# Set-up of a gated expert layer: matrix products moved from VectorE to GpSimd, TensorE and ScalarE

## The reference, cut to what matters

```
x = x + ga * attn(layernorm(x) * (1 + ca) + sa)        # 8 batches of 1024 tokens, width 128, 8 heads
h = layernorm(x) * (1 + cb) + sb
x = x + gb * ffn(h)

def ffn(h):
    gates = softmax over the 2 best of 8 experts of h[:, 0, :] @ Wr.T     # one row of gates per batch
    mid = einsum('blh,erh->belr', h, A)
    expert_out = einsum('belr,ehr->belh', mid, Bw)
    return h + einsum('be,belh->blh', gates, expert_out)
```

## Time and profile before

| | us |
|---|---|
| median of 3 runs | 816.1 (813.3 to 819.37) |
| the profiled execution, its own time | 814.3 |
| its span | 812.5 |
| mean granted TensorE clock in it | 0.958 of full speed |

### The profile page before, as it was taken

The page is one execution under the profiler, slowest core; times in us unless marked ns, Lnnn a source line. Parts: engine busy times, 40 slices in busy tenths (PEclk is TensorE's granted clock), DMA queues, the critical chain, the costliest instruction groups (busy, mean ns, idle before and its releaser), DMA issues.

```text
span 812.5 us, 21167 instructions
## 1 busy us (share of the span) xinstructions
PE 705.3 (87%) x4437; PEld 577.8 (71%) x4437; DVE 759.0 (93%) x6490; ACT 678.9 (84%) x2182; POOL 465.8 (57%) x871
## 2 busy tenths in 40 slices
PE   5987989999898889988988899889888998898844
PEld 3445667777777777777777777777777777777743
DVE  5956899999999999999999999999999999999980
ACT  3981359988888998898989988898999888988964
POOL 2112456666666666666666666666666666666541
PEclk9995989999999999999999999999999999999955
DMA  5310000111111001111110011111100111111000
GB/s 171 107 31 10 25 17 27 32 32 32 33 31 31 27 26 32 32 32 32 31 31 27 26 32 33 33 31 31 31 25 29 32 31 32 32 31 31 19 4 10
DMA packets 49232, 27.23 MB, mean 34 GB/s; under 512 B 5513, under 2 KB 48593, under 8 KB 49105
## 3 DMA queue, kind: packets, MB, share of 16 engines
q1 hardware_dynamic: 49104, 25.90, 10.9%
HBM read 10.28 MB, written 4.19 MB: 18 GB/s over the span
## 4 chain that ended last, share of the span: by engine, by line
DVE 83%; PE 9%; ACT 2%; DMA 2%; issue 1%; POOL 1%; SPq 1%; ACTq 0%; POOLq 0%
DVE work L990 46%; DVE m L979 30%; DVE key L1012 5%; DMA big<-in_x 1%; PE psD L1145 1%; DVE key L801 1%; PE psD L1050 1%; DVE st_p L792 1%; PE psC L1175 1%; PE psC L1078 1%; PE psW L1232 1%; PE psW L1161 1%; DMA wmod_sb<-in_wmod 1%; POOL big L452 1%; PE psX L1133 0%
## 5 line engine op out<-in xcount | busy, mean ns | idle before, releaser
L990 DVE MATCH_REPLACE8 work<-m,work 128x64 f32<-128x64 f32 x1536 | 301.0, 208 | 0.0
L1145 PE MATMUL psD<-sst,tst 128*128 128x224 f32 x1024 | 238.7, 356 | 0.0
L979 DVE MAX8 m<-work 128x8 f32<-128x64 f32 x1536 | 211.5, 210 | 0.0
L1145 PEld LDWEIGHTS psD<-sst,tst 128*128 128x128 f32 x1024 | 196.5, 192 | 3.1 <-issue 0.3
L452 POOL TENSOR_TENSOR big<-work,con 128x512 f32<-128x512 f32 x128 | 162.2, 1290 | 20.5 <-ACT work L635 15.9
L481 POOL TENSOR_TENSOR t<-cst,qh 128x128 f32<-128x128 f32 x64 | 27.7, 433 | 213.2 <-ACT cst L715 213.2
L1175 PE MATMUL psC<-vst,big 128*128 128x34 f32 x1024 | 127.5, 270 | 0.0
L1175 PEld LDWEIGHTS psC<-vst,big 128*128 128x128 f32 x1024 | 126.8, 195 | 0.2
L990 DVE MATCH_VALUE_LOAD work<-m,work 128x8 f32 x1536 | 122.3, 80 | 0.0
L990 DVE MATCH_REPLACE8 work<-m,key 128x64 f32<-128x64 f32 x512 | 100.2, 208 | 0.0
L1142 PE MATMUL psD<-mask_bf,ident_bf 128*128 128x448 bf16 x256 | 91.5, 357 | 1.8 <-DMA tst<-nst 1.8
(11 more groups left out here) (200 smaller groups left out, 1473.6 us busy)
## 6 DMA issues: line engine op xcount, KB each, us to landing
hst<-hT_all SPq DMA_DIRECT2D x64, 96.0 KB
tst<-qT_all SPq DMA_DIRECT2D x256, 17.0 KB
big<-in_x SPq DMA_DIRECT2D x16, 256.0 KB, 2.8
tst<-nst SPq DMA_DIRECT2D x256, 1.0 KB
xs<-in_x SPq DMA_DIRECT2D x64, 64.0 KB, 1.9
out<-yo SPq DMA_DIRECT2D x64, 64.0 KB, 1.7
sst<-nst SPq DMA_DIRECT2D x128, 3.0 KB
con<-in_consts SPq DMA_DIRECT2D x1, 549.5 KB, 6.7
```

Of the source, the lines that this page charges most:

```text
L979: last = v.max(m8[:, h], src[:, h * WIN:(h + 1) * WIN])
L990: last = v.match_replace(work[:, s, cols], m8[:, h], src[:, cols], GONE)
L1145: last = mm(bank_of(r)[:, g, 0:SW], tst[:, s, r, g], sst[:, s, g], start=False, stop=(g == NG - 1), skip_group_check=True)
```

## The change

- DVE: both `bsc` products, and `expert_matrices` with both its calls, are taken out.
- POOL: `routing(0)` makes all four `bsc`. In `step(1)`, after `unfold(1)`, it multiplies the two halves of `g_b` by `mI`, each after the copy on ACT.
- PE: `routing(0)` adds the identity by one more product per bank (identity by identity repeated four times, 128 x 512).
- ACT: `routing(1)` copies the two banks to `mI`, 128 x 512 each, ahead of its `step(1)`.
- `mI` has room for both halves. PE's `contexts(0)` of step 1 waits for the two copies; the wait for `gb_ready` moves to the first use of `g_b`, in step 3.

```
--- before.py
+++ after.py
@@ buffers and semaphores
-        mI = sb("mI", [P, 4, D])
+        mI = sb("mI", [P, 2, 4, D])
+        mI_ready = sem("mI_ready")
@@ POOL, step(i), behind unfold(1)
+                if i == 1:
+                    for half in range(2):
+                        four = slice(4 * half, 4 * half + 4)
+                        pool.wait_ge(mI_ready, half + 1)
+                        nc.gpsimd.tensor_tensor(g_b[:, four], g_b[:, four], mI[:, half], ALU.mult).then_inc(gb_ready, 1)
@@ POOL, routing(0)
-                    for kt in range(2, 4):
+                    for kt in range(4):
                         nc.gpsimd.tensor_tensor(bsc[:, kt], b_sb[:, kt].unsqueeze(1).broadcast_to([P, NB, D]),
@@ ACT, routing(i)
+                if i == 1:
+                    for half, bank in enumerate((psC, psX)):
+                        act.wait_ge(pG_ready, half + 1)
+                        nc.scalar.activation(mI[:, half].rearrange("p b d -> p (b d)"), bank[:], ACT.Copy).then_inc(mI_ready, 1)
@@ DVE, routing(i)
-                if i == 0:
-                    dve.wait_ge(r0_dve, 10)
-
-                    for kt in range(2):
-                        v.tensor_tensor(bsc[:, kt], b_sb[:, kt].unsqueeze(1).broadcast_to([P, NB, D]),
-                                        gate_er[:, kt].unsqueeze(2).broadcast_to([P, NB, D]), ALU.mult).then_inc(bsc_ready, 1)
-                if i == 1:
-                    expert_matrices(0)
-
-            def expert_matrices(half):
-
-                four = slice(4 * half, 4 * half + 4)
-                dve.wait_ge(pG_ready, half + 1)
-                need(dve, gb_ready, half)
-                link(v.tensor_tensor(mI[:], (psC, psX)[half][:].rearrange("p (b d) -> p b d", b=4),
-                                     ident.unsqueeze(1).broadcast_to([P, 4, D]), ALU.add))
-                v.tensor_tensor(g_b[:, four], g_b[:, four], mI[:], ALU.mult).then_inc(gb_ready, 1)
@@ DVE, step(i), behind replaces(i, 0, 1)
-                if i == 1:
-                    expert_matrices(1)
@@ PE, routing(0)
                         for kt in range(4):
-                            last = mm(bank[:], a_sb[:, kt], bsc[:, kt, 4 * half:4 * half + 4].rearrange("p b d -> p (b d)"),
-                                      start=(kt == 0), stop=(kt == 3))
-                        last.then_inc(pG_ready, 1)
+                            mm(bank[:], a_sb[:, kt], bsc[:, kt, 4 * half:4 * half + 4].rearrange("p b d -> p (b d)"),
+                                      start=(kt == 0), stop=False)
+                        mm(bank[:].rearrange("p (b d) -> p b d", b=4), ident, ident.unsqueeze(1).broadcast_to([P, 4, D]),
+                           start=False, stop=True).then_inc(pG_ready, 1)
@@ PE, contexts(0) of step 1
-                                pe.wait_ge(gb_ready, 2)
+                                pe.wait_ge(mI_ready, 2)
@@ PE, step(i), ahead of the product with g_b
+                    if k == 0:
+                        pe.wait_ge(gb_ready, 2)
```

## The result

Over 22 runs each, the changed kernel's median is 816.19 us (814.12 to 820.77) and that of the kernel before 813.67 (811.07 to 819.37). The ratio is 1.0036, with a 95% interval of 1.0018 to 1.0053: 2.9 us slower by this ratio and by the means of the runs, 2.5 us between the two medians, clear of noise, and far from 1%. The forecast was +0.3%.

A forecast was written before the change was run, and what follows sets the result against it. The chain over PE, ACT and POOL, not DVE, bounds the stretch up to chunk 3's L1012. Identity 1.71 + copies 1.10 - unfold 0.44 = 2.37 us; 816.1 + 2.4 = 818.5 us, range 813.0 to 823.0.

The forecast's parts named there:

- DVE has slack, the chain over PE, ACT and POOL bounds the stretch: From 92.33 us to chunk 3's L1012 at 120.84, the 8.3 us taken off DVE all turn into waits.
- The rival of 807.8: DVE is the bound throughout, so its 8.3 us are gained: 816.1 - 8.3 = 807.8 us; chance 0.04.
- bsc on POOL at 1.75 to 1.90 each, free: Four in routing(0) end at 90.6 to 91.2, before PE's first expert product at 92.33; cost 0.
- the -0.44 of the unfold: POOL's first pair of unfolds takes 2.54 for 2.98 us, without DVE's L969 in between.
- estimate of 2.25 us for one bsc: Price on POOL from the skill's 4497 ns for 2048 elements; 0.3 us of wait on PE; not taken.
- Identity 1.71: Two more fp32 products of 0.86 us on PE, before its step 0 on the chain: +1.71 us.
- Copies 1.1: ACT's two bank copies, behind L772 and ahead of L628, go into the chain: 1.0 to 1.2, taken 1.1 us.
- Products with mI covered by POOL's wait: Two behind unfold(1), 2.1 to 3.0 us, covered by POOL's 3.04 us wait for ACT's cst; cost 0.
- The clock as before: PE's fall to 1.2 GHz at 108.65 to 115.40 us stays; up to 2.6 us less or more otherwise.
- DVE's waits 5.0 and 2.5 at chunks 2 and 3: DVE waits 5.0 us for L686 at chunk 2 and 2.5 us at chunk 3's L1012.
- Its signs: Right: DVE busy 8.4 us less, chunk 3's L1012 at 123.2. Wrong: PE's first expert product after 93, among others.

The follow-up runs named there:

- e12: Kernel before with the identity added by PE as in the change and DVE copying the banks where it added; ratio 1.0048 to the kernel before.
- e9: The changed kernel once more, unedited, for a second trace and median; ratio 1.0033 to the kernel before.
- e1: Kernel before with all four bsc products on POOL and none on DVE, nothing else moved; ratio 1.0004 to the kernel before.
- e7: Kernel before with one more 128x512 fp32 product on PE, result unused, in its wait for POOL at the head of step 1; ratio 0.9979.
- e3: Changed kernel with PE's two identity products moved to the end of routing(-1), where PE waits for a DMA; ratio 1.0012 to the kernel before.

## Why the prediction was right

Time, range and direction held: +2.4 us forecast, +2.9 measured, and 816.19 lies in 813 to 823. The forecast of 818.5 stood on a median of 3 runs that was 2.4 above the one of 22; the ratio is what it got right (1.0029 for 1.0036), and the median itself was missed by 2.3. By its steps:

- *DVE has slack, the chain over PE, ACT and POOL bounds the stretch.* Right, and shown from both sides: 5.2 us less DVE work alone change nothing (37.08 for 37.24), 8 us more in the changed kernel change nothing (41.07 for 41.08). The rival of 807.8 is out.
- *bsc on POOL at 1.75 to 1.90 each, free.* Right: each 1.895 or 1.896, 7.46 us for four, 1.2 us ahead of PE. The reading of the durations as turns between DVE and POOL gave the price; their mean of 2.39 would not have. It also bore out the -0.44 of the unfold: 2.52 for 2.98, and 2.50 in e12, where DVE's product with mI ends before the unfold begins. The prediction's estimate of 2.25 us for one bsc was too long: 1.90 is measured. The 4497 ns behind it stand in the Trainium skill, "GPSIMD Engine Reference", in "3.1 Elementwise — side-by-side cycle accounting", and not in the section that the prediction names. The Trainium skill, "SBUF — State Buffer", "Who interferes with whom", has it that a DVE instruction with at most one SBUF input, outside the 2-port modes, doesn't contend with POOL; the trace agrees, as none of the four is longer than another beside DVE's L1003, MAX8 and MATCH_REPLACE8.
- *Identity 1.71.* Right: 1.71 in the change, alone, and by leaving it out.
- *Copies 1.1.* 0.95, just under its bounds of 1.0 to 1.2.
- *Products with mI covered by POOL's wait.* Right: 2.52 us for the two, and L488 (L481 before) still waits. I had said that this wait would nearly go; 1.9 us of it are left, as the low clock on the contexts makes ACT's cst later. POOL's timeline of the changed kernel, to be read against the earlier trace rows:

```profile
110.21 2.52 POOL L476 TENSOR_TENSOR g_b<-g_b,mI 128x512 f32<-128x512 f32 x2
112.66 0.84 POOL L482 TENSOR_TENSOR sqs<-qT_all 128x384 f32<-128x384 f32 x1
115.39 0.43 POOL L488 TENSOR_TENSOR t<-cst,qh 128x128 f32<-128x128 f32 x1 [1.88 <-ACT cst L726]
```

- *The clock as before.* The one weak step. The terms without it give 1.71 + 0.95 - 0.46 = 2.2; the second trace's 2.41 is near that, the first's 3.84 is not. Of the 1.6 between, 1.4 lie in PE's rows at half clock (10 us of it for 6.75). In the second trace the nearness is a balance: the fall comes ahead of the contexts there too and costs 1.0 us in them and the transposes, and step 1 gives 1.0 back (5.23 us for 6.27), as the full clock returns within it. I had put up to 2.6 for that into the range and nothing into the value.
- *DVE's waits 5.0 and 2.5 at chunks 2 and 3.* 4.77 and 3.86; the second carries the clock's share.
- *Its signs.* One of those for wrong came up: the first expert product starts after 93 (93.11). POOL is not the cause, its last bsc ends at 91.89; chunk 0's L1012 is 0.8 us later in this execution, 84.40 for 83.60. DVE's busy time fell by 7.9 us, for 8.4 forecast.

That the clock explains the rest of the measured 2.9 us is argued, not shown. Each run's mean granted clock, over the whole span, speaks against so simple an account: beside e9, on one chip, the 19 of 35 runs of the kernel before with 0.963 or more have a median of 812.0 us, the other 16 of 815.7, and 11 of the 12 runs of the changed kernel with 0.963 or more have 816.2. Among these the change costs some 4 us, and the traces of the kernel before and of its two nearest variants (e1, e7), all three with the fall at the contexts, are of executions with 0.962 or less. What the stretch takes in the more frequent ones, no trace shows. So the path and its terms were right, and how near 2.4 came to 2.9 is in part luck.

## What to carry to other kernels

The busiest engine over the span need not bound the stretch where a change acts: ask who arrives last at the first point behind it that never waits again, and only take work off the chain that ends there. Where work moves to engines of that chain, its place in their in-order programs decides its price: the same two copies cost 0.95 us behind a wait and nothing ahead of it, and the same two products 1.7 us in the chain, and less than nothing in a wait of PE. With both put there, the kernel is some 0.2% faster than before (0.998 and 0.9982, both intervals reach 1) instead of 0.36% slower.

## What the runs showed of the hardware

- A 1.8 us wait of PE filled with two products kept PE at 2.4 GHz through the next step in all four traces that have it; with the wait empty the clock fell behind it in all ten that don't. The first expert product then came 1.2 us sooner in the program.
- One program, unedited, was granted 1.2 GHz for 10 us in one trace and for some 7 in another, at the same place; the difference from chunk 0 to chunk 3 was 1.4 us. A wait of 1.68 us in front of the transposes had the fall behind it in the changed kernel and none in e3.
- DVE and POOL taking turns is worth a look in both directions: without a two-input product of DVE beside it a 128x384 product on POOL went from 1.80 to 0.83 us, and a pair of unfolds from 2.98 to 2.52.
